# One-hot operands of an expert layer read from PSUM, and three GpSimd steps moved out of its dense part

## The chip, the cores and the metric

The kernel runs on one core of a Trainium2 chip. The metric is the time of one execution on the device, in microseconds (us). The engines are the matrix engine (PE), VectorE (DVE), ScalarE (ACT), GpSimd (POOL) and SyncE (SP), which issues the transfers. Each has a program of its own, and they meet through semaphores. PE, DVE and ACT reach PSUM, where the matmuls write; POOL works on SBUF alone.

## What is computed

A layer of phase attention on x (2 x 4096 tokens, 256 features) is followed by a layer of 16384 small experts. The second one is what matters here:

```
x  = x + layernorm(attention(layernorm(x)))
xn = layernorm(x)
q  = xn @ Wq + bq                        # 8 heads, two halves of 32 each
v1, i1 = top_k(q1 @ K1.T, 10); v2, i2 = top_k(q2 @ K2.T, 10)
vals, best = top_k(v1[:, None] + v2[None, :], 10)
expert_idx = (i1 * 64 + i2)[best]
h  = gelu(xn . W_down[expert_idx]) * softmax(vals)
x  = x + layernorm(sum(h * W_up[expert_idx]))
```

## The kernel before

The attention phase comes first and ends near 0.8 ms. `experts_phase` then takes the 8192 tokens in 32 chunks of C = 256. Its loop is a software pipeline that each engine's program writes out by hand: iteration m runs the dense layer of chunk m, builds the gate matrix of chunk m + 1, makes the lists of chunk m + 2 and starts chunk m + 3. What an engine's loop body says in which order is the order in which it works.

No expert is gathered. The indices that occur lie below 4096, and each is split into a number q (128 values, NQ) and a number r (32 values, NR). The dense layer computes all experts for all tokens of the chunk in 16 pairs of r: `down` on PE (12 matmuls a pair, into one of two banks, `hbank[p % 2]`), `gelu` on ACT from that bank into `hid`, `mix` on POOL, which multiplies by the gates, and `up` on PE, three pairs later. x and the weights are split into a high and a low part for `down`, hence `xT_hi` and `xT_lo`.

The gates of a chunk come from one-hots over its 80 slots (8 heads x 10): for each token, PE multiplies a one-hot of q (`ohq`, 80 x 128) with one of r that carries the gate (`ohr`, 80 x 32, a high and a low part). The 256 tokens are four blocks of 64. The q one-hots of block 0 are made by POOL (`onehots`, 13 pieces beside the pairs), those of block 1 by ACT, those of blocks 2 and 3 by DVE (`onehots_q`, 8192 elements a partition). DVE makes all r one-hots (`onehots_r`: a comparison, a product with `ghi`, a product with `glo`, 2048 elements each). A comparison sets a number per token against `q_no`, a row of the numbers 0 to 127. All of it is fp16.

In iteration m DVE runs, in this order: the moments of chunk m + 3, `decode` of chunk m + 1 (splits the indices, and makes the factors of POOL's one-hots), the lists of m + 2 (`lists_first`, `lists_rest`, `pair_sums`, whose first sum has 160 elements, `pairs_top`, `shift`, `mask`, `product`), then `onehots_r` and `onehots_q` of m + 1 with `finish` and `norm_out` of m between them, and `soften`. PE runs the dense layer, then the queries and scores of m + 3, and the four blocks of gate matmuls; block b waits for DVE's r one-hots of that block.

POOL runs `root(0, m + 3)` (a reciprocal root for the input's norm, two instructions on 2 elements a partition), then the 16 pairs: `mix`, and beside it `add_input` (the residual of chunk m - 1) at pair 0, `low_x` (x's low part, chunk m + 2) at pair 1, `norm_in` (the norm itself, chunk m + 3) at pair 2, `low_gates` at pair 5, `numbers` and `pair_numbers` at pair 10, and a piece of `onehots` in each of 13. At the end it runs `root(1, m)`, for the output's norm.

Of the kernel before, what the change touches and what calls it, by code (L numbers as in the profile page):

```python
# [5 lines left out]
F32, F32R, F16, BF16, U16 = mybir.dt.float32, mybir.dt.float32r, mybir.dt.float16, mybir.dt.bfloat16, mybir.dt.uint16  # L6
# [16 lines left out]
BLOCKS = 4  # L23
# [772 lines left out]
def experts_phase(nc, ctx, sems, chunks, x1_dram, out_dram, w, x1_written):  # L796
# [77 lines left out]


    consts_in, wq_in, wdown_in, wup_in, x1_in, x1t_in, out_done = (
        sem(f"b_{n}") for n in ("consts_in", "wq_in", "wdown_in", "wup_in", "x1_in", "x1t_in", "out"))
# [16 lines left out]
        sem(f"b_{n}") for n in ("q_no", "eid", "fields", "qid", "id16", "oh16"))  # L894
    ohr_eq_done, ohr_hi_done, ohr_lo_done, ohq_done = (sem(f"b_{n}") for n in ("ohr_eq", "ohr_hi", "ohr_lo", "ohq"))

    xT_done, xT_hi_done, q_done, score_done, exp_done, picked_done, gateT_done, ghi_done = (
        sem(f"b_{n}") for n in ("xT", "xT_hi", "q", "score", "exp", "picked", "gateT", "ghi"))
    gates_done, wd_hi_done, gelu_done, rid_done, minus_qid_done, distance_done, ohq_act_done = (
        sem(f"b_{n}") for n in ("gates", "wd_hi", "gelu", "rid", "minus_qid", "distance", "ohq_act"))  # L900

# [88 lines left out]
    def pool_program(pool):  # L990
# [51 lines left out]
        def low_gates(m):  # L1042
            pool.wait_ge(ghi_done, m + 1)
            if m:
                pool.wait_ge(ohr_lo_done, BLOCKS * m)
            G.tensor_tensor(glo[:, :, :], twice(gateT[:, :]), ghi[:, :, :], ALU.subtract).then_inc(glo_done, 1)
# [23 lines left out]
        for m in range(-3, chunks + 1):  # L1070
            if has(m + 3):
                root(0, m + 3)

            if m in (-2, -1):
                for p in range((m + 2) * PAIRS_R // 2, (m + 3) * PAIRS_R // 2):
                    low_down(p)
            for p in range(PAIRS_R):
                if has(m):
                    mix(m, p)
                if p == 0 and has(m - 1):  # L1080
                    add_input(m - 1)
                if p == 1 and has(m + 2):
                    low_x(m + 2)
                if p == 2 and has(m + 3):
                    norm_in(m + 3)
                if p == AT_GLO and has(m + 1):
                    low_gates(m + 1)
                if p == AT_CID and has(m + 2):
                    numbers(m + 2)
                    pair_numbers(m + 2)  # L1090
                if p < POOL_PARTS and has(m + 1):
                    onehots(m + 1, p)
            if has(m):
# [142 lines left out]
    def act_program(act):  # L1236
# [29 lines left out]
        def turn_gates(m):  # L1266
            act.wait_ge(gate_pe, m + 1)
            if m:
                act.wait_ge(glo_done, m)
            S.mul(gateT[:, :], mbank[1][0:SLOTS, 0:C], GATE_SCALE).then_inc(gateT_done, 1)  # L1270
            act.wait_ge(gateT_done, m + 1)
            if m:
                act.wait_ge(ohr_hi_done, BLOCKS * m)
            S.copy(ghi[:, :, :], gateT[:, :].unsqueeze(2).to_broadcast([SLOTS, C, 2])).then_inc(ghi_done, 1)
# [25 lines left out]
        def soften(m):  # L1300
# [50 lines left out]
        for m in range(-3, chunks + 1):  # L1351
# [30 lines left out]
    def dve_program(dve):  # L1382
# [8 lines left out]
        def onehots_q(m, b):  # L1391
            tok = slice(b * BLK, (b + 1) * BLK)
            shape = [SLOTS, BLK, NQ // 2, 2]
            dve.wait_ge(q_no_done, 1)
            dve.wait_ge(qid_done, m + 1)
            if m:
                dve.wait_ge(gates_pe, GROUPS * m)
            V.tensor_tensor(ohq[:, tok, :].rearrange("p n (q s) -> p n q s", s=2),  # L1398
                            qid[:, tok, :].unsqueeze(2).to_broadcast(shape),
                            q_no[0:SLOTS, :].rearrange("p (q s) -> p q s", s=2).unsqueeze(1).to_broadcast(shape),  # L1400
                            ALU.is_equal).then_inc(ohq_done, 1)

# [188 lines left out]
        for m in range(-3, chunks + 1):  # L1591
# [106 lines left out]
```

## Time and profile before

| | before |
|---|---|
| median of 3 executions | 3560.59 us (3557.9 to 3568.86) |
| profiled execution | 3565.71 us, span 3563.9 us |
| busy | PE 3177.3 us (89%), DVE 3086.5 (87%), ACT 2120.2 (59%), POOL 1935.4 (54%) |
| mean granted clock of PE | 0.891 |

The span runs from the first to the last instruction of the profiled execution. Busy shares are means over two phases with different limits: in the expert phase alone the page shows PE and DVE in nine tenths or more of nearly every slice.

### The profile page before, as it was taken

How to read it: one execution, taken by the hardware profiler on the slowest of the kernel's cores; microseconds unless marked ns; L12 is line 12 of the kernel's file. 1: busy time of each engine (PE TensorE's matmuls, PEld its weight loads, DVE VectorE, ACT ScalarE, POOL GpSimd, SP SyncE). 2: the span in 40 equal slices, each digit the busy share in tenths (PEclk: the TensorE clock that was granted, in tenths of full speed). 3: DMA queues.
4: the chain of work that ended last, by engine and by line, in shares of the span. 5: the costliest groups of instructions: out<-in, count | busy, mean ns of one | idle time of the engine just before them, and what ended most of it. 6: DMA issues, size and time to landing. Idle time of an engine off the chain costs nothing. (4 is left out here: it accounts for less than half of the span.)

```text
span 3563.9 us, 91251 instructions
## 1 busy us (share of the span) xinstructions
PE 3177.3 (89%) x31284; PEld 2733.0 (77%) x31284; DVE 3086.5 (87%) x15020; ACT 2120.2 (59%) x4411; POOL 1935.4 (54%) x1758
## 2 busy tenths in 40 slices
PE   5999999972599999999999999999999999999988
PEld 3666666642488888888888888888888888888878
DVE  5666666656999999999999999999999999999971
ACT  3444444422666666666666766666666666766662
POOL 1333333333466666556556666666556656666664
PEclk9999999986699988988888999889998888999988
DMA  2111111103333333333333333333333333333332
GB/s 64 48 54 54 54 54 54 42 30 133 141 117 117 116 105 114 122 105 105 105 105 118 125 119 119 117 108 105 124 112 105 105 105 115 124 124 117 114 117 95
DMA packets 132328, 356.85 MB, mean 100 GB/s; under 512 B 13865, under 2 KB 61609, under 8 KB 129452
## 3 DMA queue, kind: packets, MB, share of 16 engines
q1 hardware_dynamic: 131868, 351.03, 30.3%
q8 instruction: 251, 4.11, 0.5%
q14 instruction: 209, 1.71, 0.2%
HBM read 309.01 MB, written 25.17 MB: 94 GB/s over the span
## 5 line engine op out<-in xcount | busy, mean ns | idle before, releaser
L1209 PE MATMUL b_ps_a<-b_wup,b_hid 128*128 128x256 f32 x4096 | 955.8, 379 | 1.5 <-POOL b_hid L1023 1.5
L1198 PE MATMUL b_ps_h<-b_xT_hi,b_wd_split 128*128 128x256 f32 x4096 | 931.9, 311 | 22.7 <-ACT b_hid L1349 22.5
L1209 PEld LDWEIGHTS b_ps_a<-b_wup,b_hid 128*128 128x128 f32 x4096 | 744.3, 190 | 85.7 <-POOL b_hid L1023 1.7
L1023 POOL TENSOR_TENSOR b_hid<-b_hid,b_gates 128x512 f32<-128x512 f32 x512 | 661.9, 1295 | 197.8 <-ACT b_hid L1349 197.8
L1198 PEld LDWEIGHTS b_ps_h<-b_xT_hi,b_wd_split 128*128 128x128 f32 x4096 | 703.5, 200 | 38.3 <-issue 27.9
L1328 ACT ACTIVATE b_ohq<-b_q_no,b_minus_qid 80x128 f16<-80x128 f16 x2048 | 648.7, 391 | 1.0
L1004 POOL TENSOR_SCALAR b_rstd<-b_mv 128x2 f32<-128x2 f32 x64 | 136.4, 2131 | 860.8 <-DVE b_mv L1388 860.8
L1123 PE MATMUL b_ps_s<-b_ohr,b_ohq 80*128 80x32 f16 x16384 | 452.6, 185 | 167.1 <-issue 125.5
L1198 PE MATMUL b_ps_h<-b_xT_lo,b_wd_split 128*128 128x256 f32 x2048 | 596.9, 291 | 0.0
L1123 PEld LDWEIGHTS b_ps_s<-b_ohr,b_ohq 80*128 80x128 f16 x16384 | 443.8, 102 | 176.0 <-issue 132.3
L1349 ACT ACTIVATE b_hid<-b_ps_h 128x512 f32<-128x512 f32 x512 | 303.8, 593 | 371.5 <-PE b_ps_h L1198 371.3
L1038 POOL TENSOR_TENSOR b_ohq<-b_qT 80x640 f16<-80x640 f16 (+1 forms) x416 | 519.8, 1250 | 0.0
L1244 ACT ACTIVATE b_gates<-b_ps_s 128x512 f32<-128x512 f32 x512 | 298.1, 595 | 245.8 <-PE b_ps_s L1123 243.9
L1198 PEld LDWEIGHTS b_ps_h<-b_xT_lo,b_wd_split 128*128 128x128 f32 x2048 | 412.0, 201 | 9.9
L1336 ACT ACTIVATE b_ohq<-b_ohq,b_one 80x1024 f16<-80x1024 f16 x256 | 291.6, 1139 | 0.1
L1398 DVE TENSOR_TENSOR b_ohq<-b_qid,b_q_no 80x8192 f16<-80x8192 f16 x64 | 284.0, 4438 | 0.2 <-issue 0.2
L240 POOL TENSOR_TENSOR a_ret<-a_prod 128x512 f32<-128x512 f32 x64 | 84.9, 1327 | 329.7 <-DVE a_prod L618 329.7
L1519 DVE TENSOR_TENSOR b_cand<-b_val 128x80 f32<-128x80 f32 (+3 forms) x160 | 219.6, 1435 | 2.9
L1485 DVE FIND_INDEX8 b_idx<-b_val,b_score 128x8 uint16<-128x64 f32 x1024 | 200.4, 218 | 0.0
L1500 DVE FIND_INDEX8 b_idx<-b_val,b_score 128x8 uint16<-128x64 f32 x1024 | 200.4, 219 | 0.0
L1492 DVE MATCH_REPLACE8 b_score<-b_val,b_score 128x64 f32<-128x64 f32 x1024 | 199.8, 209 | 0.0
L480 ACT COPY a_carry<-a_ps_c 32x512 f32<-32x512 f32 x128 | 68.0, 576 | 216.9 <-PE a_ps_c L336 216.7
(192 smaller groups left out, 5508.8 us busy)
## 6 DMA issues: line engine op xcount, KB each, us to landing
b_wd_split<-wd_parts SPq DMA_DIRECT2D x512, 512.0 KB, 3.8
a_keysh<-a_key SPq DMA_DIRECT2D x16, 896.0 KB, 5.4
a_x<-in_x SPq DMA_DIRECT2D x16, 512.0 KB, 4.9
x_between<-a_y SPq DMA_DIRECT2D x16, 512.0 KB, 3.2
b_x<-x_between SPq DMA_DIRECT2D x32, 256.0 KB, 2.7
wd_parts<-b_wd_split SPq DMA_DIRECT2D x16, 512.0 KB, 2.9
b_x1t<-x_between SPq DMA_DIRECT2D x32, 256.0 KB, 5.5
out<-b_y SPq DMA_DIRECT2D x32, 256.0 KB, 5.6
```

The lines of the kernel that those rows point to most:

```text
L1023: G.tensor_tensor(hid[:, p % 4, :, :], hid[:, p % 4, :, :], gates[:, 2 * p:2 * p + 2, :], ALU.mult).then_inc(mix_done, 1)
L1038: G.tensor_tensor(ohq[:, tok, :].rearrange("p n (a b) -> p n a b", a=16), oh16[:, tok, :].unsqueeze(3).to_broadcast(shape), oh8[:, tok, :] ...
L1123: mm = T.matmul(bank[:, n * NR:(n + 1) * NR], ohq[:, tok, :], ohr[:, b % 2, tok - b * BLK, part, :], start=part == 0, stop=part == 1)
L1198: mm = T.matmul(hbank[p % 2][:, j * C:(j + 1) * C], a, c, start=i == 0, stop=i == len(parts) - 1)
L1209: mm = T.matmul(abank[:, t * D:(t + 1) * D], hid[:, p % 4, j, t * P:(t + 1) * P], wup[:, 2 * p + j, :], start=p == 0 and j == 0 and t == 0 ...
L1244: S.mul(gates[:, :, g * GROUP:(g + 1) * GROUP], sbank[fills["gates", m, g] % 3][:, :].rearrange("p (n r) -> p r n", r=NR), 1.0 / GATE_SCAL ...
L1328: op = S.activation(ohq[:, BLK + i, :], q_no[0:SLOTS, :], ACT.Abs, bias=minus_qid[:, i:i + 1])
L1336: S.activation(rows, rows, ACT.Relu, bias=one[:, :], scale=-1.0).then_inc(ohq_act_done, 1)
L1349: S.activation(hid[:, p % 4, :, :], hbank[p % 2][:, :].rearrange("p (j c) -> p j c", j=2), ACT.Gelu).then_inc(gelu_done, 1)
L1398: V.tensor_tensor(ohq[:, tok, :].rearrange("p n (q s) -> p n q s", s=2), qid[:, tok, :].unsqueeze(2).to_broadcast(shape), q_no[0:SLOTS, :] ...
L1485: op = V.max_index(idx[:, t, l, 0:8], val[:, t, l, 0:8], src(l))
L1519: op = V.tensor_tensor(cand[:, :, off:off + na * nb].rearrange("p h (a b) -> p h a b", a=na), v[:, :, 0, a0:a0 + na].unsqueeze(3).to_broad ...
```

## The change

DVE's one-hots take their small operands from PSUM in place of SBUF. The two banks of `down` are free once the activations of a chunk are done, so a part of the first one receives a copy of `q_no` (`keep_q_numbers`, on DVE, once per chunk) and the second one copies of `ghi` and `glo` (`keep_gate_parts`, on ACT, after `turn_x`). The copies move 4-byte words, and the one-hots read them as fp16. On POOL the norm of the input (`norm_in`) moves right behind its root, ahead of the dense layer; `low_x` moves behind the 16 pairs and takes chunk m + 3; `add_input` moves behind `root(1, m)` and takes chunk m.

```diff
+    q_no_ps = hbank[0][0:SLOTS, :].bitcast(F16)[:, 0:NQ]
+    gate_ps = [hbank[1][0:SLOTS, :].bitcast(F16)[:, i * 2 * C:(i + 1) * 2 * C].rearrange("p (n s) -> p n s", s=2) for i in range(2)]
...
         def low_gates(m):
             pool.wait_ge(ghi_done, m + 1)
             if m:
-                pool.wait_ge(ohr_lo_done, BLOCKS * m)
+                pool.wait_ge(gate_ps_done, m)
...
             if has(m + 3):
                 root(0, m + 3)
+                norm_in(m + 3)
...
-                if p == 0 and has(m - 1):
-                    add_input(m - 1)
-                if p == 1 and has(m + 2):
-                    low_x(m + 2)
-                if p == 2 and has(m + 3):
-                    norm_in(m + 3)
...
+            if has(m + 3):
+                low_x(m + 3)
             if has(m):
                 root(1, m)
+                add_input(m)
...
-            if m:
-                act.wait_ge(ohr_hi_done, BLOCKS * m)
             S.copy(ghi[:, :, :], gateT[:, :].unsqueeze(2).to_broadcast([SLOTS, C, 2])).then_inc(ghi_done, 1)
...
+        def keep_gate_parts(m):
+            act.wait_ge(glo_done, m + 1)
+            if m:
+                act.wait_ge(gelu_done, PAIRS_R * m)
+
+            for i, part in enumerate((ghi, glo)):
+                op = S.copy(hbank[1][0:SLOTS, i * C:(i + 1) * C], part[:, :, :].rearrange("p n s -> p (n s)").bitcast(F32))
+            op.then_inc(gate_ps_done, 1)
...
             if has(m + 3):
                 turn_x(m + 3)
+            if has(m + 1):
+                keep_gate_parts(m + 1)
+            if has(m + 3):
                 queries(m + 3)
...
-            dve.wait_ge(q_no_done, 1)
+            dve.wait_ge(q_no_ps_done, m + 1)
...
-                            q_no[0:SLOTS, :].rearrange("p (q s) -> p q s", s=2).unsqueeze(1).to_broadcast(shape),
+                            q_no_ps.rearrange("p (q s) -> p q s", s=2).unsqueeze(1).to_broadcast(shape),
                             ALU.is_equal).then_inc(ohq_done, 1)
...
+        def keep_q_numbers(m):
+            dve.wait_ge(q_no_done, 1)
+            if m:
+                dve.wait_ge(gelu_done, PAIRS_R * m - 1)
+            V.tensor_copy(hbank[0][0:SLOTS, 0:NQ // 2], q_no[0:SLOTS, :].bitcast(F32)).then_inc(q_no_ps_done, 1)
...
-            dve.wait_ge(glo_done, m + 1)
-            V.tensor_tensor(hi, lo, ghi[:, tok, :].unsqueeze(2).to_broadcast(shape), ALU.mult).then_inc(ohr_hi_done, 1)
+            dve.wait_ge(gate_ps_done, m + 1)
+            V.tensor_tensor(hi, lo, gate_ps[0][:, tok, :].unsqueeze(2).to_broadcast(shape), ALU.mult).then_inc(ohr_hi_done, 1)
             dve.wait_ge(ohr_hi_done, n + 1)
-            V.tensor_tensor(lo, lo, glo[:, tok, :].unsqueeze(2).to_broadcast(shape), ALU.mult).then_inc(ohr_lo_done, 1)
+            V.tensor_tensor(lo, lo, gate_ps[1][:, tok, :].unsqueeze(2).to_broadcast(shape), ALU.mult).then_inc(ohr_lo_done, 1)
...
             if has(m + 1):
+                keep_q_numbers(m + 1)
                 onehots_r(m + 1, 0)
```

On POOL, from one iteration into the next, there stands before: the root of the output (L1004 and L1007, of which the last one is the first row), the root of the next input, and then the pairs with their guests (`mix` is L1023, `onehots` L1038).

```order
L1007 TENSOR_TENSOR b_rstd<-b_rstd,b_minus_half 128x2
L1004 TENSOR_SCALAR b_rstd<-b_mv 128x2
L1007 TENSOR_TENSOR b_rstd<-b_rstd,b_minus_half 128x2
L1023 TENSOR_TENSOR b_hid<-b_hid,b_gates 128x512
L1012 TENSOR_TENSOR b_y<-b_y,b_x1t 128x512
L1038 TENSOR_TENSOR b_ohq<-b_qT 80x640
L1023 TENSOR_TENSOR b_hid<-b_hid,b_gates 128x512
L997 TENSOR_TENSOR b_xT_lo<-b_xT,b_xT_hi 128x512
L1038 TENSOR_TENSOR b_ohq<-b_qT 80x640
L1023 TENSOR_TENSOR b_hid<-b_hid,b_gates 128x512
L1028 TENSOR_SCALAR b_x1<-b_x1,b_mv,b_rstd 128x256 x2
```

And in the changed kernel, from the last three products of an iteration on (`mix` is L1028 there, `onehots` L1043, `low_x` L1002, `add_input` L1017, `norm_in` L1033).

```order
L1028 TENSOR_TENSOR b_hid<-b_hid,b_gates 128x512 x3
L1002 TENSOR_TENSOR b_xT_lo<-b_xT,b_xT_hi 128x512
L1009 TENSOR_SCALAR b_rstd<-b_mv 128x2
L1012 TENSOR_TENSOR b_rstd<-b_rstd,b_minus_half 128x2
L1017 TENSOR_TENSOR b_y<-b_y,b_x1t 128x512
L1009 TENSOR_SCALAR b_rstd<-b_mv 128x2
L1012 TENSOR_TENSOR b_rstd<-b_rstd,b_minus_half 128x2
L1033 TENSOR_SCALAR b_x1<-b_x1,b_mv,b_rstd 128x256 x2
L1028 TENSOR_TENSOR b_hid<-b_hid,b_gates 128x512
L1043 TENSOR_TENSOR b_ohq<-b_qT 80x640
```

The residual, x's low part and the norm have left the pairs and stand around them, four instructions in all.

On DVE, behind `product` (L1569), there stands before the first r block and the start of the second: a comparison (L1412), the product with the high part (L1417) and with the low part (L1419).

```order
L1569 TENSOR_TENSOR b_score<-b_score,b_cid 128x4320
L1412 TENSOR_TENSOR b_ohr<-b_rid,b_q_no 80x64x32
L1417 TENSOR_TENSOR b_ohr<-b_ohr,b_ghi 80x64x32
L1419 TENSOR_TENSOR b_ohr<-b_ohr,b_glo 80x64x32
L1412 TENSOR_TENSOR b_ohr<-b_rid,b_q_no 80x64x32
```

And in the changed kernel (`product` is L1590 there).

```order
L1590 TENSOR_TENSOR b_score<-b_score,b_cid 128x4320
L1422 COPY b_ps_h<-b_q_no 80x64
L1433 TENSOR_TENSOR b_ohr<-b_rid,b_ps_h 80x64x32
L1438 TENSOR_TENSOR b_ohr<-b_ohr,b_ps_h 80x64x32
L1440 TENSOR_TENSOR b_ohr<-b_ohr,b_ps_h 80x64x32
```

The copy is new, and one of the two inputs of each one-hot is now `b_ps_h`, a bank of PSUM, in the other r blocks and in the q one-hots too. Nothing else of DVE's order moves: the same instructions follow each other, with the copy ahead of the first r block.

## Rows read from the trace of the kernel before

Rows of a timeline give the start in us, the duration in us, the engine, the line, the operation with output and inputs, and the idle time before it in brackets with what ended it. Rows of groups end in count, busy us, mean ns of one, and idle time before them.

**Rows 1.** Windows: stretch, length, busy us and instructions by engine, clock, DMA

```profile
1869.54:1951.99 82.45, 76.44 (x891) 70.50 (x888) 81.19 (x432) 55.77 (x123) 51.10 (x46) 0.89 0.36 113
1923.30:1951.99 28.69, 23.61 (x560) 21.26 (x559) 28.21 (x36) 17.33 (x29) 6.79 (x4) 0.75 0.13 47
```

**Rows 2.** Timeline of PE at the end of one iteration

```profile
1944.03 3.58 PE L1123 MATMUL b_ps_s<-b_ohr,b_ohq 80*128 80x32 f16 x128 [2.78 <-issue]
1948.58 3.57 PE L1123 MATMUL b_ps_s<-b_ohr,b_ohq 80*128 80x32 f16 x128 [0.97 <-issue]
1951.99 0.56 PE L1198 MATMUL b_ps_h<-b_xT_hi,b_wd_split 128*128 128x256 f32 x1
```

**Rows 3.** Timelines of DVE, first and twelfth of thirty such rows

```profile
990.59 6.14 DVE L1519 TENSOR_TENSOR b_cand<-b_val 128x160 f32<-128x160 f32 x1
...
1898.77 6.50 DVE L1519 TENSOR_TENSOR b_cand<-b_val 128x160 f32<-128x160 f32 x1
```

**Rows 4.** Timeline of POOL beside the last row

```profile
1898.88 1.29 POOL L1023 TENSOR_TENSOR b_hid<-b_hid,b_gates 128x512 f32<-128x512 f32 x1
...
1905.16 0.35 POOL L1054 TENSOR_SCALAR b_id<-b_idx 128x160 f16<-128x160 uint16 x1
```

**Rows 5.** Groups of DVE by line and shape, 1200 to 3500 us

```profile
L1398 DVE TENSOR_TENSOR b_ohq<-b_qid,b_q_no 80x8192 f16<-80x8192 f16 x56 | 248.8, 4443 | 0.2 <-issue 0.2
L1519 DVE TENSOR_TENSOR b_cand<-b_val 128x160 f32<-128x160 f32 x27 | 171.8, 6364 | 2.4
...
L1412 DVE TENSOR_TENSOR b_ohr<-b_rid,b_q_no 80x2048 f16<-80x2048 f16 x113 | 140.0, 1239 | 3.7 <-issue 3.7
...
L1446 DVE TENSOR_TENSOR b_qT<-b_field,b_q_no 80x512 f16<-80x512 uint16 x28 | 19.1, 680 | 0.0
...
L1519 DVE TENSOR_TENSOR b_cand<-b_val 128x80 f32<-128x80 f32 x54 | 17.2, 318 | 0.0
```

**Rows 6.** Timeline of POOL during a q one-hot of DVE

```profile
1936.07 4.29 POOL L1004 TENSOR_SCALAR b_rstd<-b_mv 128x2 f32<-128x2 f32 x1 [17.97 <-DVE b_mv L1388]
```

**Rows 7.** Timeline of DVE beside a run of L1017 on POOL

```profile
885.15 1.74 DVE L1446 TENSOR_TENSOR b_qT<-b_field,b_q_no 80x512 f16<-80x512 uint16 x1
```

**Rows 8.** Groups of DVE in the first phase, 0 to 750 us

```profile
L605 DVE TENSOR_TENSOR a_u<-a_cs,a_ps_p 128x512 f32<-128x512 f32 x62 | 42.1, 678 | 7.0 <-PE a_ps_p L306 4.2 <-issue 2.7
...
L564 DVE TENSOR_TENSOR a_wg<-a_key,a_wg 128x1024 fp32r<-128x1024 f32 x1 | 1.2, 1218 | 0.0
...
L564 DVE TENSOR_TENSOR a_wb<-a_key,a_wb 128x256 fp32r<-128x256 f32 x1 | 0.4, 416 | 0.0
```

**Rows 9.** Groups of POOL by line and shape, 1200 to 3500 us

```profile
L1028 POOL TENSOR_SCALAR b_x<-b_x,b_mv,b_rstd 128x256 f32<-128x256 f32 x52 | 63.4, 1226 | 0.0
L1012 POOL TENSOR_TENSOR b_y<-b_y,b_x1t 128x512 f32<-128x512 f32 x28 | 37.3, 1331 | 0.0
L997 POOL TENSOR_TENSOR b_xT_lo<-b_xT,b_xT_hi 128x512 fp32r<-128x512 f32 x27 | 34.3, 1271 | 0.0
```

**Rows 10.** Timelines of ACT, then POOL: activation and product of pair 9

```profile
1979.60 0.60 ACT L1349 ACTIVATE b_hid<-b_ps_h 128x512 f32<-128x512 f32 x1 [0.35 <-PE b_ps_h L1198]
...
1983.70 1.27 POOL L1023 TENSOR_TENSOR b_hid<-b_hid,b_gates 128x512 f32<-128x512 f32 x1
```

**Rows 11.** Timeline of POOL at the start of an iteration

```profile
1950.69 0.72 POOL L1007 TENSOR_TENSOR b_rstd<-b_rstd,b_minus_half 128x2 f32<-128x2 f32 x1
```

**Rows 12.** Timelines of ACT, then DVE, around the end of the dense layer

```profile
1916.16 0.60 ACT L1349 ACTIVATE b_hid<-b_ps_h 128x512 f32<-128x512 f32 x1 [0.35 <-PE b_ps_h L1198]
...
1918.94 0.62 ACT L1257 CAST b_xT_hi<-b_xT 128x512 fp32r<-128x512 f32 x1
1925.23 0.84 ACT L1287 ACTIVATE b_qT<-b_ps_s,b_bq 128x256 f32<-128x256 f32 x2 [5.67 <-PE b_ps_s L1173]
...
1918.55 2.41 DVE L1560 TENSOR_TENSOR b_score<-b_posf,b_pair_no 128x4320 f16<-128x4320 f16 x1
```

**Rows 13.** Timeline of DVE, iteration before the last

```profile
3487.65 0.76 DVE L1459 BATCH_NORM_STATS2 b_stat<-b_ps_a 128x6 f32<-128x256 f32 x2 [14.70 <-PE b_ps_a L1209]
```

More of the change, by code:

```diff
@@ L894, in experts_phase @@
         sem(f"b_{n}") for n in ("q_no", "eid", "fields", "qid", "id16", "oh16"))
-    ohr_eq_done, ohr_hi_done, ohr_lo_done, ohq_done = (sem(f"b_{n}") for n in ("ohr_eq", "ohr_hi", "ohr_lo", "ohq"))
+    ohr_eq_done, ohr_hi_done, ohr_lo_done, ohq_done, q_no_ps_done = (
+        sem(f"b_{n}") for n in ("ohr_eq", "ohr_hi", "ohr_lo", "ohq", "q_no_ps"))
     xT_done, xT_hi_done, q_done, score_done, exp_done, picked_done, gateT_done, ghi_done = (
         sem(f"b_{n}") for n in ("xT", "xT_hi", "q", "score", "exp", "picked", "gateT", "ghi"))
-    gates_done, wd_hi_done, gelu_done, rid_done, minus_qid_done, distance_done, ohq_act_done = (
-        sem(f"b_{n}") for n in ("gates", "wd_hi", "gelu", "rid", "minus_qid", "distance", "ohq_act"))
+    gates_done, wd_hi_done, gelu_done, rid_done, minus_qid_done, distance_done, ohq_act_done, gate_ps_done = (
+        sem(f"b_{n}") for n in ("gates", "wd_hi", "gelu", "rid", "minus_qid", "distance", "ohq_act", "gate_ps"))
     xT_pe, q_pe, score_pe, picks_pe, picked_pe, gate_pe, gates_pe, down_pe, up_pe = (
@@ L1405, in onehots_r @@
             n = BLOCKS * m + b
-            dve.wait_ge(q_no_done, 1)
+            dve.wait_ge(q_no_ps_done, m + 1)
             dve.wait_ge(rid_done, m + 1)
@@ L1412, in onehots_r @@
             V.tensor_tensor(lo, rid[:, tok, :].unsqueeze(2).to_broadcast(shape),
-                            q_no[0:SLOTS, 0:NR].rearrange("p (r s) -> p r s", s=2).unsqueeze(1).to_broadcast(shape),
+                            q_no_ps[:, 0:NR].rearrange("p (r s) -> p r s", s=2).unsqueeze(1).to_broadcast(shape),
                             ALU.is_equal).then_inc(ohr_eq_done, 1)
             dve.wait_ge(ohr_eq_done, n + 1)
-            dve.wait_ge(glo_done, m + 1)
-            V.tensor_tensor(hi, lo, ghi[:, tok, :].unsqueeze(2).to_broadcast(shape), ALU.mult).then_inc(ohr_hi_done, 1)
+            dve.wait_ge(gate_ps_done, m + 1)
+            V.tensor_tensor(hi, lo, gate_ps[0][:, tok, :].unsqueeze(2).to_broadcast(shape), ALU.mult).then_inc(ohr_hi_done, 1)
             dve.wait_ge(ohr_hi_done, n + 1)
-            V.tensor_tensor(lo, lo, glo[:, tok, :].unsqueeze(2).to_broadcast(shape), ALU.mult).then_inc(ohr_lo_done, 1)
+            V.tensor_tensor(lo, lo, gate_ps[1][:, tok, :].unsqueeze(2).to_broadcast(shape), ALU.mult).then_inc(ohr_lo_done, 1)
         def decode(m):
```

## The prediction

> **What bounds the kernel now.** I read the windows first. Of the span of 3563.9 us the expert phase takes more than three quarters, and in its steady part one iteration of the loop (one chunk of 256 tokens) lasts 82.45 us, with VectorE (DVE) busy for 81.19 and the matrix engine (PE) for 76.44 [rows 1]. A busy share that high says little alone, so I asked who waits for whom. In the timeline PE waits 2.78 and 0.97 us ahead of the third and fourth block of gate matmuls, which read what DVE's one-hots write, and the dense layer of the next chunk can only start behind the fourth, at 1951.99 [rows 2]. DVE's one-hots and sums have next to no idle time ahead of them (0.2 to 3.7 us over 28 iterations, [rows 5]). So DVE's own list of instructions, end to end, sets the period, and PE would need 82.45 - 2.78 - 0.97 = 78.7 us.
>
> DVE's list holds one thing that is no work. The first sum of candidate values, 160 numbers, takes 6.50 us in the shown iteration and 6.14 in the first of thirty such rows [rows 3]; the group's mean is 6.364 us, while the next sum, of 80 numbers, takes 0.318 [rows 5]. I take the latter as its real length. While it stands there GpSimd (POOL) runs five instructions without a gap, and the sum ends just after POOL has reached L1054, where its run breaks [rows 4]. DVE is being held off by POOL: about 6.364 - 0.318 = 6.05 us of each iteration. It goes the other way too: a POOL instruction on four numbers takes 4.29 us where it starts beside a q one-hot of 4.443 us [rows 5, 6]. And where POOL runs a row of L1017, a DVE instruction that takes 0.680 us elsewhere takes 1.74 [rows 5, 7]: here DVE gets a turn after one POOL instruction, at 1.06 us each. All these DVE instructions read two tensors from SBUF. The Trainium skill, SBUF — State Buffer, section Who interferes with whom, states that a DVE instruction with two SBUF inputs contends with a POOL instruction that reads SBUF, and one with at most one such input does not; these rows agree with the first half, and none shows the second for a two-tensor operation.
>
> **The change, part by part.** Times below lie on the shown iteration.
>
> *POOL's dense-layer work.* Three pieces leave it: L1012 (1.331 us), L997 (1.271) and two of L1028 (1.226 each), together 5.05 us [rows 9]. Today POOL is late: the activation of pair 9 ends at 1980.20, the product on it starts at 1983.70, 3.5 us later [rows 10]. POOL needs about 1.26 us an instruction (five between 1898.88 and 1905.16), 2.5 us a pair; PE and ACT deliver a pair every 3.17 us (pair 9 at 1979.60, an iteration earlier at 1897.15; pair 15 at 1916.16, six pairs on) [rows 4, 10, 12]. Without 5.05 us of other work, about one of which turns into waiting for the first activations, POOL is level at pair 9, and from there it idles 0.7 us in each pair. That is where DVE's candidate sum arrives. Its hold-off shrinks from 6.05 us to what is left of one pair of POOL instructions, between 0 and 2.5; I take one turn, 1.06.
>
> *The input's norm* now runs straight behind the root at the start of the iteration. POOL's L1007 ends at 1951.41 [rows 11], and DVE is then in its decode, whose last four instructions read two SBUF tensors. Two POOL instructions fall on them. By the turn of [rows 7] that costs DVE 2 x 1.06 = 2.1 us that it doesn't pay today. Bounds: 0, and 2 x 1.226 = 2.45.
>
> *A knock-on at the end of the dense layer.* DVE reaches L1560 at 1918.55 today, when POOL is done [rows 12]. It will be there about 6.05 - 3 x 1.06 = 2.9 us sooner, at 1915.7, and run until 1918.1. The last activation ends at 1916.76 [rows 12]; POOL's product on it then queues behind L1560 and takes its turn before L1569, another two-input instruction. One more turn of 1.06 (0 to 1.27).
>
> *x's low part and the residual.* Low x waits for ACT's copy at 1919.56 [rows 12] and falls behind L1569 at the worst; nothing reads it until a later chunk. The residual runs during the last r one-hots. Both cost 0 if those one-hots, with one input now in PSUM, don't contend; if they do, 1.06 to 1.27 each.
>
> *The one-hots.* Fourteen an iteration: 2 of L1398, and 12 of L1412, L1417 and L1419. No row shows a two-byte tensor read from PSUM. The nearest: in the first phase 256 and 1024 fp32 elements take 0.416 and 1.218 us from SBUF, so 0.149 + 1.044 ns an element, which gives 0.684 for 512; the same width with one input in PSUM took 0.678 [rows 8]. So where an operand lies costs nothing there. L1412 takes 1.239 us for 2048 elements, 0.6 ns each: two-byte tensors pass two at a time [rows 5]. I take both to stay: 0 extra. The upper bound is that they pass singly, below.
>
> *The copies.* DVE copies 64 words of numbers to PSUM ahead of the first one-hot, which waits for it: 0.2 us, bounded by 0 and the 0.318 of an 80-element sum [rows 5]. ACT copies the two parts of the gates, at most 0.62 each by its nearest copy, ahead of a wait of 5.67 us for the queries [rows 12], so hidden. They are done at 1919.56 + 1.24 = 1920.8, and DVE's first multiplication, at about 1924.7 today (L1560's start plus two of 2.41 and one of 1.24), will come at about 1923. It doesn't wait. If that cover went it would cost the difference.
>
> *The end.* In the iteration before the last DVE makes one-hots early and then idles 14.70 us for PE [rows 13]. Now they must wait for the dense layer, since its banks hold their operands. The chain after the dense layer there grows by two r blocks and a q block, 6 x 1.24 + 4.44 = 11.9 us [rows 5], less some 8 that fit beside its last pairs (an estimate): about 4 us, once.
>
> *Sum.* 6.05 - 1.06 - 2.1 - 1.06 - 0.2 = 1.6 us an iteration, 30 times (the count in rows 3): 48 us, less 4 is 44. The profiled execution took 3565.7 us, 5.1 above the median 3560.6, so I expect about 3521 for a profiled one and **3517** for the median. The new period is 80.8, above PE's 78.7, so DVE still sets it.
>
> **The rivals.**
> *PE becomes the bound.* If the new collisions mostly miss (POOL idle when DVE comes), DVE falls to 82.45 - 6.05 + 0.2 = 76.6 and PE's 78.7 decides: 3.75 x 30 = 112, less 4: 3452. Half-way cases lie at 3480 to 3500. For it: POOL's gaps of 0.7 in a pair. Against it: the norm and the decode both start from the same event, so these two must meet. The chance of anything from 3452 to 3500: 0.28.
> *The bills eat the gain.* With all upper bounds, 2.5 + 2.45 + 1.27 + 0.3 = 6.5 of the 6.05, the time is 3560.6 + 0.45 x 30 + 4 = 3578. This fits if DVE is passed over for more than one turn, as in rows 3. Between 3550 and 3580: 0.18, about half of it within 0.3%.
> *A two-byte operand in PSUM passes one element at a time.* Then L1398 takes 0.149 + 8192 x 1.044 ns = 8.70 us and L1412 2.29: 2 x 4.26 + 12 x 1.05 = 21.1 us an iteration, 32 chunks: 675 us, so 3517 + 675 = 4190. It decides as soon as the one-hots, 23.8 us an iteration, grow by more than 1.5 us, 6%. Against it: the fp32 row of [rows 8], which could not show it. The chance: 0.10.
> The Trainium skill, VectorE: DVE Perf Modes, speaks for this rival: the perf-mode tier table there gives tensor_tensor one element per cycle with any PSUM operand. The section Why PSUM operands drop a tier, on the same page, leaves two-byte data two per cycle. No row here settles it.
> *The change does not free POOL* (another wait holds the candidate sum): then only the new bills show, 3578 to 3600; 0.03, since the sum ends with POOL's run in all thirty rows.
>
> **How the numbers follow.** The forecast, 3500 to 3550, has 0.41. A difference under 0.3%, 11 us, is about what a measurement of this kernel can't tell from none. Faster: 0.41 + 0.28 = 0.69; the same: 0.11; slower: 0.20, half of it by the PSUM rate. The range takes all bounds but the far cases: 3455 to 3565.
>
> **What would show it.** In the profile after, the candidate sum of 160 should average 1.4 us instead of 6.364; the decode's two-input instructions should take about 2 us more in sum; L1560 should start near 1.2 us before the last activation ends, and L1569 or the product be 1 us long in excess; L1398 should stay at 4.44 and L1412 at 1.24 (8.7 and 2.3 mean the third rival); L1004 should fall from 4.29 to about 0.2 beside a q one-hot; PE's waits ahead of the third and fourth block should shrink but not vanish. I'm wrong if the turns are longer than one POOL instruction, or if PSUM's rate is lower.

## The result, and the profile after

The median fell from 3560.64 us (3557.9 to 3568.86, four executions) to 3501.7 (3500.14 to 3502.66, four): a ratio of 0.9824 with a 95% interval of 0.9812 to 0.9836. I had said 3517, so the sign held, and the gain, 59 us, was larger than the 44 of the sum. The mechanism of the gain held too, but two terms of the sum were off by the same 1.9 us in opposite directions, as the last parts show.

The quickest way to see where it came from is one instruction that runs once per chunk. The fused field operation of `decode` is L1440 before and L1461 after. The views of those two lines (count, shortest, median and longest duration in ns, first and last start in us), before and after:

```profile
L1440 DVE SCALAR_TENSOR_TENSOR b_id<-b_eid,b_field x32: 278/280/1347, 883.9 to 3431.1; 80x128 f16<-80x128 uint16 x32
```

```profile
L1461 DVE SCALAR_TENSOR_TENSOR b_id<-b_eid,b_field x32: 279/281/282, 883.8 to 3363.8; 80x128 f16<-80x128 uint16 x32
```

Over 31 chunks 2547.2 us became 2480.0: a mean period of 82.17 against 80.00, 2.17 less. From the last start to the end of the span it was 132.8 and is 136.3, 3.5 us more. The two spans differ by 63.8 us, the medians by 59: the profiled execution of the kernel before lay 5 us above its median.

The windows of a steady iteration and of its tail (columns as in [rows 1]):

```profile
1843.02:1923.25 80.23, 76.42 (x886) 70.47 (x887) 77.00 (x433) 56.38 (x126) 51.13 (x47) 0.90 0.36 116
1895.00:1923.25 28.25, 25.42 (x569) 22.87 (x568) 25.90 (x34) 17.38 (x30) 3.86 (x6) 0.78 0.17 58
```

PE and POOL are busy as long as in [rows 1] (76.42 against 76.44, 51.13 against 51.10), and PE's granted clock is 0.90 against 0.89; VectorE's busy time fell from 81.19 to 77.00. But 80.23 - 77.00 leaves 3.2 us in which DVE is not shown busy, where before there were 1.3. The groups of DVE say which lines shrank, which grew, and where it now waits (columns as in [rows 5], 1200 to 3350 us):

```profile
L1412 DVE TENSOR_TENSOR b_ohq<-b_qid,b_ps_h 80x8192 f16<-80x8192 f16 x54 | 237.4, 4397 | 0.0
...
L1433 DVE TENSOR_TENSOR b_ohr<-b_rid,b_ps_h 80x2048 f16<-80x2048 f16 x106 | 128.5, 1213 | 51.1 <-PE b_ps_s L1126 50.1
...
L1590 DVE TENSOR_TENSOR b_score<-b_score,b_cid 128x4320 f16<-128x4320 f16 x27 | 90.9, 3368 | 0.9
...
L1540 DVE TENSOR_TENSOR b_cand<-b_val 128x80 f32<-128x80 f32 x54 | 39.1, 724 | 0.0
...
L1471 DVE TENSOR_TENSOR b_qT<-b_id,b_q_no 80x1024 f16<-80x1024 f16 x27 | 23.6, 872 | 0.0
...
L1540 DVE TENSOR_TENSOR b_cand<-b_val 128x160 f32<-128x160 f32 x27 | 13.2, 490 | 2.8 <-issue 0.4
```

The candidate sum of 160 fell from 6364 ns [rows 5] to 490. The two sums behind it grew from 318 to 724 each: part of the hold-off has moved onto them. L1590, `product`, takes 3368 ns and took 2443. The one-hots take as long with an operand in PSUM: 4397 against 4443 ns, 1213 against 1239. But [rows 5] reach to 3500 us and so into the last iterations; in the window used here the kernel before has 4402 ns for the q one-hot, 2408 for `product`, 6423 for the sum of 160, and for the r comparison

```profile
L1412 DVE TENSOR_TENSOR b_ohr<-b_rid,b_q_no 80x2048 f16<-80x2048 f16 x105 | 127.4, 1213 | 0.0
```

So where the operand lies changed nothing for the one-hots there. And L1433, the r comparison, waits 50.1 us for PE's gate matmuls: a wait that the kernel before did not have.

The timeline of POOL shows what stands beside the shorter sum (columns as in [rows 4]):

```profile
1871.18 1.28 POOL L1028 TENSOR_TENSOR b_hid<-b_hid,b_gates 128x512 f32<-128x512 f32 x1 [0.47 <-ACT b_hid L1360]
1872.41 1.34 POOL L1043 TENSOR_TENSOR b_ohq<-b_qT 80x640 f16<-80x640 f16 x1
1874.34 1.28 POOL L1028 TENSOR_TENSOR b_hid<-b_hid,b_gates 128x512 f32<-128x512 f32 x1 [0.58 <-ACT b_hid L1360]
...
1886.95 2.99 POOL L1028 TENSOR_TENSOR b_hid<-b_hid,b_gates 128x512 f32<-128x512 f32 x1 [1.22 <-ACT b_hid L1360]
1890.10 3.24 POOL L1028 TENSOR_TENSOR b_hid<-b_hid,b_gates 128x512 f32<-128x512 f32 x1 [0.17 <-ACT b_hid L1360]
...
1905.11 0.22 POOL L1009 TENSOR_SCALAR b_rstd<-b_mv 128x2 f32<-128x2 f32 x1 [10.53 <-DVE b_mv L1402]
...
1922.55 3.34 POOL L1033 TENSOR_SCALAR b_x<-b_x,b_mv,b_rstd 128x256 f32<-128x256 f32 x2
```

POOL now waits for each activation by pair 9, half a microsecond a pair, where before it ran 3.5 us behind [rows 10]. The five sums, from 1872.25 to 1874.26, lie between two of those gaps and last 2.01 us. The fourth and fifth row are products that stretch from 1.28 to about 3 us: DVE holds them. The root beside a q one-hot takes 0.22 us in its row and took 4.29 [rows 6]. The last row is the moved norm, two instructions in 3.34 us.

DVE beside these rows, in time order: the five candidate sums as one row, `product`, the copy, a q one-hot, the r comparison of block 2, and the end of `decode`:

```profile
1872.25 2.01 DVE L1540 TENSOR_TENSOR b_cand<-b_val 128x160 f32<-128x160 f32 x5
...
1888.84 3.37 DVE L1590 TENSOR_TENSOR b_score<-b_score,b_cid 128x4320 f16<-128x4320 f16 x1
1892.13 0.22 DVE L1422 COPY b_ps_h<-b_q_no 80x64 f32<-80x64 f32 x1
...
1904.93 4.38 DVE L1412 TENSOR_TENSOR b_ohq<-b_qid,b_ps_h 80x8192 f16<-80x8192 f16 x1
1911.25 1.22 DVE L1433 TENSOR_TENSOR b_ohr<-b_rid,b_ps_h 80x2048 f16<-80x2048 f16 x1 [1.93 <-PE b_ps_s L1126]
...
1922.38 0.56 DVE L1458 SCALAR_TENSOR_TENSOR b_qid<-b_eid 80x384 f16<-80x384 uint16 x1
1922.86 0.28 DVE L1461 SCALAR_TENSOR_TENSOR b_id<-b_eid,b_field 80x128 f16<-80x128 uint16 x1
1923.06 0.68 DVE L1467 TENSOR_TENSOR b_qT<-b_field,b_q_no 80x512 f16<-80x512 uint16 x1
1923.66 0.88 DVE L1471 TENSOR_TENSOR b_qT<-b_id,b_q_no 80x1024 f16<-80x1024 f16 x1
```

The row at 1911.25 is the new wait: DVE is done with the q one-hots at 1909.3 and stands for 1.93 us. `onehots_r` has two buffers, and block 2's has to be given back by PE's block 0. PE comes to that block only after the dense layer, the queries and the scores, and there it stops once more for ACT. The timeline of PE, as in [rows 2]:

```profile
1906.23 2.56 PE L1126 MATMUL b_ps_s<-b_ohr,b_ohq 80*128 80x32 f16 x96
1910.12 4.41 PE L1126 MATMUL b_ps_s<-b_ohr,b_ohq 80*128 80x32 f16 x160 [1.33 <-ACT b_gates L1247]
1915.07 3.58 PE L1126 MATMUL b_ps_s<-b_ohr,b_ohq 80*128 80x32 f16 x128 [0.54 <-issue]
1919.61 3.57 PE L1126 MATMUL b_ps_s<-b_ohr,b_ohq 80*128 80x32 f16 x128 [0.96 <-issue]
1923.02 0.56 PE L1201 MATMUL b_ps_h<-b_xT_hi,b_wd_split 128*128 128x256 f32 x1
```

PE's waits ahead of its third and fourth block fell from 2.78 and 0.97 [rows 2] to 0.54 and 0.96. So each engine waits for the other: PE for the fourth r block, DVE for the buffer of the third.

### The profile page after: what moved, and what is told of

Read it like the earlier page. It is cut to its first block and busy times, and to the rows that moved or that the text cites. A ratio compares the mean times of both kernels' runs of the same rounds, so it can differ in the third digit from the quotient of the medians.

```text
span 3500.1 us, 91378 instructions
## 1 busy us (share of the span) xinstructions
PE 3179.7 (91%) x31284; PEld 2737.6 (78%) x31284; DVE 2952.2 (84%) x15052; ACT 2138.9 (61%) x4475; POOL 1916.9 (55%) x1758
## 5 line engine op out<-in xcount | busy, mean ns | idle before, releaser
L1028 POOL TENSOR_TENSOR b_hid<-b_hid,b_gates 128x512 f32<-128x512 f32 x512 | 768.3, 1501 | 182.9 <-ACT b_hid L1360 182.5
L1043 POOL TENSOR_TENSOR b_ohq<-b_qT 80x640 f16<-80x640 f16 (+1 forms) x416 | 520.4, 1252 | 0.0
L1009 POOL TENSOR_SCALAR b_rstd<-b_mv 128x2 f32<-128x2 f32 x64 | 14.1, 221 | 518.1 <-DVE b_mv L1402 518.1
L1412 DVE TENSOR_TENSOR b_ohq<-b_qid,b_ps_h 80x8192 f16<-80x8192 f16 x64 | 281.4, 4397 | 0.0
L1017 POOL TENSOR_TENSOR b_y<-b_y,b_x1t 128x512 f32<-128x512 f32 x32 | 40.7, 1273 | 303.6 <-DVE b_y L1489 303.6
L1433 DVE TENSOR_TENSOR b_ohr<-b_rid,b_ps_h 80x2048 f16<-80x2048 f16 x128 | 155.2, 1213 | 57.1 <-PE b_ps_s L1126 56.0
```

The source lines that it names most:

```text
L1028: G.tensor_tensor(hid[:, p % 4, :, :], hid[:, p % 4, :, :], gates[:, 2 * p:2 * p + 2, :], ALU.mult).then_inc(mix_done, 1)
L1043: G.tensor_tensor(ohq[:, tok, :].rearrange("p n (a b) -> p n a b", a=16), oh16[:, tok, :].unsqueeze(3).to_broadcast(shape), oh8[:, tok, :] ...
```

## The experiments

**Each half alone.** The first kernel keeps the PSUM operands and puts POOL's order back; the second keeps POOL's new order and puts the one-hots' operands back into SBUF.

```diff
 e1: on top of the changed kernel
             if has(m + 3):
                 root(0, m + 3)
-                norm_in(m + 3)
...
+                if p == 0 and has(m - 1):
+                    add_input(m - 1)
+                if p == 1 and has(m + 2):
+                    low_x(m + 2)
+                if p == 2 and has(m + 3):
+                    norm_in(m + 3)
...
-            if has(m + 3):
-                low_x(m + 3)
             if has(m):
                 root(1, m)
-                add_input(m)
 e2: the same lines the other way, on top of the kernel before
```

> The changed kernel with POOL's order as it was before: only the operands of the one-hots lie in PSUM. Theory A (the gain comes from what left the dense layer on POOL): the candidate sum is held for 6 us again, the one-hots save at most 0.04 us each, so 3550 to 3565 us, about the time before. Theory B (the gain comes from the PSUM operands, since DVE and POOL then share less): 3510 us or less, and a candidate sum well under 6 us.

> The kernel before with only the three moves on POOL, all operands in SBUF. Theory A: the candidate sums fall to about 2 us in sum of five, as in the changed kernel. The residual now falls on the last r one-hots and low x on the first ones, which read two SBUF inputs and so can be held for one POOL instruction, about 1 us each; one of these is hidden in DVE's wait of 1.93 us for PE. So 3505 to 3535 us. Theory B: little changes, 3550 us or more.

The PSUM operands alone: 3576.84 (3570.47 to 3580.54), a ratio of 1.0041 (1.0027 to 1.0055), slightly slower than before. The moves alone: 3528.31 (3522.2 to 3529.85), 0.9905 (0.9889 to 0.9922). So 32 us come from the moves, 59 from both, and the PSUM operands cost 16 alone. In e1 two DVE groups tell it:

```profile
L1542 DVE TENSOR_TENSOR b_cand<-b_val 128x160 f32<-128x160 f32 x26 | 167.1, 6427 | 2.7 <-issue 0.4
...
L1592 DVE TENSOR_TENSOR b_score<-b_score,b_cid 128x4320 f16<-128x4320 f16 x26 | 62.6, 2408 | 0.9
```

The candidate sum is held as before, and `product` isn't held. What is left is the copy and the later start of the last chunk's one-hots. The time is a miss of the expectation, which ended at 3565; the attribution comes back to it. In e2 the sum of 160 is short, as in the changed kernel (685 ns), and the bill is at the one-hots and at the POOL steps that now lie beside them; groups of DVE, then of POOL:

```profile
L1415 DVE TENSOR_TENSOR b_ohr<-b_ohr,b_ghi 80x2048 f16<-80x2048 f16 x104 | 176.6, 1698 | 3.6
L1410 DVE TENSOR_TENSOR b_ohr<-b_rid,b_q_no 80x2048 f16<-80x2048 f16 x104 | 154.4, 1484 | 2.5 <-PE b_ps_s L1121 0.5
```

```profile
L997 POOL TENSOR_TENSOR b_xT_lo<-b_xT,b_xT_hi 128x512 fp32r<-128x512 f32 x26 | 58.5, 2248 | 0.0
L1012 POOL TENSOR_TENSOR b_y<-b_y,b_x1t 128x512 f32<-128x512 f32 x26 | 55.1, 2118 | 81.9 <-DVE b_y L1466 81.9
```

With both inputs in SBUF the two kinds of r one-hot take 1698 and 1484 ns in the mean; with one in PSUM they take 1217 and 1213. That is 4 x (0.481 + 0.271) = 3.0 us an iteration which the moves alone cost and the PSUM operands save. In a timeline of e2 it is three turns of about 1 us: the last product of `mix` and then `low_x` fall on the first two instructions of block 0, and the residual on one of block 3. The net gain of the operands on top of the moves is smaller, 80.97 - 80.00 = 0.97 us in the mean period (L1438 of e2 starts from 878.1 to 3388.3), since the changed kernel also pays the copy, 0.2, and the wait for the r buffer, 1.9, which e2 hardly has (2.5 us in all). POOL's low part takes 2248 ns there and 1272 in the changed kernel. This is the second half of the rule that the prediction cited from the Trainium skill (SBUF — State Buffer, section Who interferes with whom), that a DVE instruction with at most one SBUF input doesn't contend. No row of before could show it; these do.

**The new wait.** e3 puts block 2's r one-hots into space of `hid`, which is free from the last `up` matmul of a chunk to the first activation of the next, and block 3's into slot 0. Block 2 then waits for no block of its own chunk, and block 3 for block 0, three ahead in place of two. e4 leaves the buffers and moves `norm_out` ahead of block 2, which only fills the wait with other work.

```diff
 e3
+    ohr2 = hid[0:SLOTS, :, :, :].rearrange("p a b c -> p (a b c)").bitcast(F16).rearrange("p (n a r) -> p n a r", n=BLK, a=2)
+    ohr_block = [ohr[:, 0], ohr[:, 1], ohr2, ohr[:, 0]]
...
-            if n >= 2:
-                dve.wait_ge(gates_pe, BLOCK_GROUPS * (n - 1))
+            if b == 3:
+                dve.wait_ge(gates_pe, BLOCK_GROUPS * (n - 2))
+            elif n >= 4:
+                dve.wait_ge(gates_pe, GROUPS * m)
 e4
-                onehots_r(m + 1, 2)
             if has(m):
                 norm_out(m)
             if has(m + 1):
+                onehots_r(m + 1, 2)
                 onehots_r(m + 1, 3)
```

> The changed kernel with the r one-hots of block 2 in the space of hid, so that DVE needs no wait for PE's gate matmuls of block 0. Theory A (the wait of 1.93 us an iteration is what took back part of DVE's gain): the wait goes, PE's own 80.2 less 0.54 and 0.96 of idle time decides, 78.7 us an iteration: 3450 to 3465 us. Theory C (DVE's instructions alone set the period, the wait only fills a gap that PE would leave anyway): 3495 to 3505 us.

> The changed kernel with norm_out ahead of the r one-hots of block 2 on DVE, so that its 0.9 us fill half of the wait for PE. Theory A: 0.9 us an iteration, 30 times, 27 us less: 3468 to 3480 us, with a wait of about 1.0 in place of 1.93. Theory C: no change, 3497 to 3505 us.

e3 took 3445.72 (3444.02 to 3447.0), 0.9673 (0.9657 to 0.9689); e4 took 3474.96 (3469.57 to 3476.96), 0.9749 (0.9733 to 0.9766). The r comparison in e3, then in e4:

```profile
L1437 DVE TENSOR_TENSOR b_ohr<-b_rid,b_ps_h 80x2048 f16<-80x2048 f16 x81 | 98.2, 1212 | 0.9
```

```profile
L1433 DVE TENSOR_TENSOR b_ohr<-b_rid,b_ps_h 80x2048 f16<-80x2048 f16 x108 | 131.0, 1213 | 27.1 <-PE b_ps_s L1126 26.2
```

Idle time ahead of it: 51.1 us in the changed kernel, 27.1 in e4, 0.9 in e3, over 26 or 27 iterations. The runs lie 27 (e4) and 56 us (e3) below the changed kernel. The periods say what of that belongs to the wait. The field operation of `decode` starts from 886.7 to 3338.5 in e4 (L1461), and in e3

```profile
L1465 DVE SCALAR_TENSOR_TENSOR b_id<-b_eid,b_field x32: 278/281/282, 875.0 to 3305.1; 80x128 f16<-80x128 uint16 x32
```

These are periods of 79.09 and 78.39 us against 80.00. In e4 the wait fell by 0.9 us and the period by 0.91; in e3 the wait of 1.9 went and the period fell by 1.61. So the buffer's wait set the period of the changed kernel, down to about 78.4, where e3 meets the next bound. Another 8.8 us of the difference between the profiled executions of e3 and the changed kernel come from the earlier start of the expert phase, 875.0 against 883.8, whose code up to there is the same. Over the nine profiles that start ranges from 875.0 to 886.7, and single profiles don't tell whether that belongs to the kernel or to the execution; the mean period is the safer number. Without the 8.8 us e3's 3445.7 would lie in the 3450 to 3465 expected; as it stands it misses that range by 4.

**Is it the norm in the dense layer?** e5 takes the changed kernel and moves only `norm_in` back to pair 2.

```diff
 e5
                 root(0, m + 3)
-                norm_in(m + 3)
...
+                if p == 2 and has(m + 3):
+                    norm_in(m + 3)
```

> The changed kernel with norm_in back at pair 2 of the dense layer, everything else as changed. Theory A (DVE's candidate sum is passed over until POOL's run of instructions breaks, so what counts is whether POOL is level with the activations by then): with 2.45 us more to do, POOL is level only behind pair 10, the sum is held for about 4.5 us, of which the wait of 1.93 us for PE and the freed holds take up 3: 3530 to 3550 us. Theory D (DVE is held for one instruction of POOL's at a time): the sum is held for one turn as now, 3497 to 3505 us.

3545.83 (3545.21 to 3551.07), a ratio of 0.9954 (0.9937 to 0.9971) to before, whose median in that group of runs was 3564.19. The sum is held again; its group, then POOL's timeline at the end of the hold in one iteration, in which DVE shows `1886.36 5.81` for the five sums:

```profile
L1541 DVE TENSOR_TENSOR b_cand<-b_val 128x160 f32<-128x160 f32 x26 | 130.0, 5001 | 2.7 <-issue 0.4
```

```profile
1886.14 1.25 POOL L1043 TENSOR_TENSOR b_ohq<-b_qT 80x640 f16<-80x640 f16 x1
1887.36 1.26 POOL L1028 TENSOR_TENSOR b_hid<-b_hid,b_gates 128x512 f32<-128x512 f32 x1
1888.58 1.25 POOL L1043 TENSOR_TENSOR b_ohq<-b_qT 80x640 f16<-80x640 f16 x1
1889.80 1.28 POOL L1028 TENSOR_TENSOR b_hid<-b_hid,b_gates 128x512 f32<-128x512 f32 x1
1891.17 0.34 POOL L1059 TENSOR_SCALAR b_id<-b_idx 128x160 f16<-128x160 uint16 x1
```

Two instructions of 1.22 us put back into the dense layer, and 4.5 us of hold-off return on the first sum; the sums of 80 are back at 316 ns, so over the five sums it is 3.8. The period rose by 1.5 only (L1462 from 879.2 to 3406.9, 81.54), since the wait of 1.9 for PE is gone. DVE reaches the candidate sum while POOL is in an unbroken run, and the run of two-tensor instructions ends at L1059, where the first sum gets through, as in [rows 4]. So in this place the hold-off is not a price per POOL instruction: it lasts as long as POOL's run, and 2.5 us decide whether POOL is still in one.

**Is DVE held in `decode`, and by what?** The prediction has the norm, started beside `decode`, hold DVE by a turn for each of its two instructions. It didn't: L1471 takes 872 ns in the mean, where the same instruction (L1450) took 680 before, and the norm is the one that is held, 1674 ns each against 1226 [rows 9]. e6 puts another POOL step there, `low_x`, a two-tensor instruction, between the root and the norm, and takes it away from the end.

```diff
 e6
                 root(0, m + 3)
+            if has(m + 2):
+                low_x(m + 2)
+            if has(m + 3):
                 norm_in(m + 3)
...
-            if has(m + 3):
-                low_x(m + 3)
```

> The changed kernel with low_x (of chunk m + 2) between the root and norm_in at the start of the iteration, where DVE decodes. Theory E (a tensor_tensor of POOL with two inputs takes a turn from DVE, the tensor_scalar of norm_in did not): a two-input instruction of the decode takes 1.06 us more; time about the same, since the wait for PE takes it up, 3497 to 3507 us. Theory F (a chain of DVE's that runs already is not broken by a POOL instruction that asks later, whatever it is): the decode takes no more than the 0.2 us it lost in the changed kernel.

3499.29 (3497.95 to 3500.64), 0.982 (0.9803 to 0.9836): the same time. The view of L1462, the field operation shown at the top, then DVE's instruction ahead of it, and the timeline of POOL beside it:

```profile
L1462 DVE SCALAR_TENSOR_TENSOR b_id<-b_eid,b_field x32: 279/1364/1370, 881.8 to 3360.9; 80x128 f16<-80x128 uint16 x32
```

```profile
1919.95 0.56 DVE L1459 SCALAR_TENSOR_TENSOR b_qid<-b_eid 80x384 f16<-80x384 uint16 x1
...
1919.98 1.66 POOL L1002 TENSOR_TENSOR b_xT_lo<-b_xT,b_xT_hi 128x512 fp32r<-128x512 f32 x1
1921.63 3.51 POOL L1033 TENSOR_SCALAR b_x<-b_x,b_mv,b_rstd 128x256 f32<-128x256 f32 x2
```

Here DVE does pay a turn: 1364 ns against 280, 1.08 us, the size of [rows 7]. And the norm behind it is again held by DVE, 3.51 us for two. Who came first doesn't tell the two cases apart. `low_x` starts 0.03 us behind a two-tensor instruction of DVE (1919.98 and 1919.95), and the norm of the changed kernel 0.17 behind the same one (1922.55 and 1922.38). What differs is the POOL instruction: the one with two tensors made DVE wait a turn, the one with a single tensor did not. This is one pair of cases, and the reason is not shown.

The time stayed for two reasons. DVE still waits 46.4 us in all for the r buffer (50.1 in the changed kernel, over the same window), so the same loop sets the period, 79.97. And the 1.08 us came back: the sums of 80 take 271 ns (724 in the changed kernel), and L1472 677 (872).

The trace of the kernel before has one more case, at the start of the expert phase, where POOL splits weights (L1017) while DVE is in `decode`:

```profile
883.44 8.69 POOL L1017 TENSOR_TENSOR b_wd_split<-b_gates,b_wd_split 128x512 fp32r<-128x512 f32 x6
```

POOL runs six two-tensor instructions here without a gap, and yet DVE's three two-tensor instructions beside them take 1.35, 1.74 and 1.74 us (starts at 883.88, 885.15 and 886.82), a turn each: the engines alternate. So a hold that lasts to the end of POOL's run is what the candidate sum shows, and not a rule for every place.

**What bounds it after the third buffer.** In e3 PE's only wait of size in the tail is 1.33 us for ACT, which exponentiates chunk m + 2 (`soften`, with two table loads) just ahead of emptying the gate banks. e8 is e3 with `soften` moved ahead of the queries, into ACT's 5.1 us of waiting.

```diff
 e8, on top of e3
             if has(m + 1):
                 keep_gate_parts(m + 1)
+            if has(m + 2):
+                soften(m + 2)
...
-            if has(m + 2):
-                soften(m + 2)
```

> The kernel with the third r buffer, and ACT's soften (an exponential and two table loads, 3.1 us) moved ahead of queries, where ACT waits 5.1 us for PE. PE's wait of 1.33 us for ACT in block 0 should go. Theory G (in the kernel with the third buffer DVE's list and PE's are nearly level, DVE at 78.4 and PE at 78.5): the period falls by 0.1 us only: 3438 to 3446 us, and PE waits about 1.2 us for DVE's one-hots again. Theory H (PE alone decides there): 77.2 us an iteration, 3405 to 3412 us.

3443.26 (3441.36 to 3448.64), 0.9667 (0.9651 to 0.9683): no different from e3. The timeline of PE in e8:

```profile
1881.84 5.34 PE L1128 MATMUL b_ps_s<-b_ohr,b_ohq 80*128 80x32 f16 x204
1887.35 3.58 PE L1128 MATMUL b_ps_s<-b_hid,b_ohq 80*128 80x32 f16 x128 [0.17 <-issue]
1891.88 3.58 PE L1128 MATMUL b_ps_s<-b_ohr,b_ohq 80*128 80x32 f16 x128 [0.96 <-issue]
```

The wait for ACT is gone, and PE waits instead for DVE's last block, 0.96 us. In e3's timeline it ran through its last two blocks without a wait. So in e3 PE and DVE are nearly level: taking 1.33 us from PE alone gives 0.23 us an iteration (the starts of L1465 run from 875.0 to 3305.1 in e3 and from 879.0 to 3302.0 in e8, 78.39 and 78.16 in the mean, one profile each). This is the kernel with the lowest median here, 121 us below the kernel before in the same group of runs, and e3 alone has nearly all of it, 115.

## Why the prediction was right, and where its terms were off

Per iteration, term by term, in the group means of before (1200 to 3500 us) and after (1200 to 3350). Means of before in the shorter window would move no term by more than 0.1:

| term | predicted | measured |
|---|---|---|
| the five candidate sums | -6.05 + 1.06 = -5.0 | 7.56 to 2.43: -5.1 |
| `decode` beside the norm | +2.1 | +0.2 |
| `product` beside the last activation's product | +1.06 | 2.443 to 3.368: +0.93 |
| the copy | +0.2 | +0.21 |
| `shift` (L1576, now L1597) | not seen | 602 to 326 ns: -0.3 |
| DVE's wait for the r buffer | not seen | 50.1 us over 27: +1.9 |
| sum | -1.6 | -2.2 |

The measured terms add up to -2.2, and the mean period fell by 2.17. Two of them show that the number came out near the forecast in part by luck: `decode` cost 1.9 us less than priced, and the wait for the r buffer, which had no price, cost 1.9. With `decode` priced right and the wait still at nothing, the sum would have been 3.5 us an iteration, a period close to PE's 78.7, and about 3460 us. The measured 3501.7 lies 1.7 us inside the forecast's 3500 to 3550. The extra gain, 15 us by the medians and 20 by the spans, comes from small terms: 0.3 us an iteration from `shift`, 0.1 each from the candidate sums and `product`, and 31 periods where the sum took 30. The "7.56" is 6.364 + 2 x 0.318 with 0.297 and 0.265 for the sums of 64 and 48 elements, the "2.43" the same lines after.

*The candidate sum*: right in mechanism and size. POOL, relieved of 5 us, is level with ACT by pair 9, as worked out; e5 shows that 2.5 us of the five already decide it. I had put the whole rest of the hold-off on the first sum (1.4 us in the mean); it is 0.49 there, and the rest lies on the sums of 80. (The POOL instruction of 4.29 us that the prediction says is on four numbers is the root, on two numbers a partition; nothing hangs on it.)

*`decode`*: this step failed. The text said, of the norm, "Two POOL instructions fall on them. By the turn of [rows 7] that costs DVE 2 x 1.06 = 2.1 us". It costs 0.2. The turn was read from a row beside L1017, an instruction with two tensors, and carried over to one that reads a single tensor. e6 puts a two-tensor one there and finds the 1.08. The range from 0 to 2.45 held it; the choice between the ends was wrong.

*`product`*: right in kind and size, but not by the instruction that I named. The last activation, and the DVE instruction that I expected to start 1.2 us before its end:

```profile
1889.43 0.60 ACT L1360 ACTIVATE b_hid<-b_ps_h 128x512 f32<-128x512 f32 x1 [0.35 <-PE b_ps_h L1201]
...
1886.39 2.41 DVE L1581 TENSOR_TENSOR b_score<-b_posf,b_pair_no 128x4320 f16<-128x4320 f16 x1
```

L1581 starts 3.6 us before that end, since DVE is earlier than the sum had it. So POOL's product of the last pair but one (the row at 1886.95) queues behind L1581 and takes its turn before L1590, which is 0.93 longer; the last pair's then waits for L1590. In e1, where POOL is still late, `product` (L1592) takes 2408.

*The copies and ACT*: right. ACT copies at 1892.73 and 1893.04 and then waits 5.10 us for the queries.

*The PSUM rate*: the third rival is out, with 4397 ns where it gave 8700. The perf-mode tier table (Trainium skill, VectorE: DVE Perf Modes), which has one element per cycle for tensor_tensor with any PSUM operand, doesn't hold for this form, two-byte elements with one operand in SBUF and one in PSUM: 2048 elements take 1.213 us here and took 1.213 from SBUF alone in the same window. The section Why PSUM operands drop a tier, which leaves two-byte data two per cycle, is the one that agrees.

*The end*: 4 us forecast, 3.5 measured. In the iteration before the last the copy waits for the activations, and a product for ACT's copies:

```profile
3409.05 0.22 DVE L1422 COPY b_ps_h<-b_q_no 80x64 f32<-80x64 f32 x1 [43.78 <-ACT b_hid L1360]
...
3413.93 1.22 DVE L1438 TENSOR_TENSOR b_ohr<-b_ohr,b_ps_h 80x2048 f16<-80x2048 f16 x1 [3.41 <-ACT b_ps_h L1316]
```

*What bounds the kernel next*: this step failed too, and it hid behind the first. I wrote "DVE still sets it", with PE's 78.7 as the next bound. With `decode` costing 0.2 instead of 2.1 DVE's own list needs 80.0 - 1.9 = 78.1 us (e3, without the wait, has a period of 78.4), and that is below a third bound that I hadn't priced: a loop over both engines, from PE's gate block 0 through the r buffer to DVE's blocks 2 and 3 and back to PE's block 3, hung onto the end of PE's scores. It stands at 80.0. All of the 1.9 us that `decode` gave was taken back there. The first rival (PE the bound, 3452 to 3500) was missed by 2 us for that reason, and e3, which takes only that loop away, lands at 3445.7. PE's wait ahead of the third block shrank as forecast, from 2.78 to 0.54; the one ahead of the fourth stayed (0.97 and 0.96).

*The attribution*: the prediction treats the two halves as one. The runs separate them: without the moves the PSUM operands gain nothing, and without the PSUM operands the moves lose 3.0 us an iteration at the one-hots. e1 took 3576.8 where 3550 to 3565 was expected. Of its 16 us above the kernel before its trace shows 10 (0.19 us in each of 31 periods and 4.2 at the end); the other 6 are not explained by any row. The two profiled executions differ by 6.1 us only: e1's expert phase starts 3.8 us earlier, its total lies 4.8 below its median, and the other's lies 5.1 above.

## What to carry to other kernels

When two engines hold each other off, the hold is not in proportion to the work beside it, so look where the other engine's run begins and ends: 2.5 us of POOL's work put back cost DVE 3.8 us at its candidate sums (e5), and 1.3 us moved elsewhere cost nothing in all (e6). Take the price of a collision only from a row where the same kind of instruction (two inputs or one, in the same place) met the same kind, and keep the full range otherwise. Before naming the next bound, go through each buffer with few slots whose writer is the engine that gets faster: its wait is at zero before and so stands in no list of waits.

## What the runs showed of the hardware

- A DVE instruction on two SBUF tensors was passed over for up to five POOL instructions in a row in the candidate sum, to the end of POOL's run (6.36 us in the mean before, 5.00 in e5), but for one only in `decode` (1.08 us in e6, and three times in a row beside the run of L1017 before). The other way round POOL's products waited for DVE's `product` (1.28 us became 3.24), and the norm for `decode` (3.34 and 3.51 for two). Why DVE gets its turn after one instruction in `decode` and not in the candidate sum no run here tells, and it stays open. In the cases with one turn DVE was already in a chain of two-tensor instructions when POOL's came, and in the long ones POOL was in its run when DVE's came; no run tests whether that decides.
- With one of its inputs in PSUM a DVE one-hot neither held POOL (0.22 us for the root, 4.29 before; 1.27 for the residual, 2.12 in e2) nor was held by it (1.21 and 1.22 us, against 1.48 and 1.70 in e2).
- The same one-hots ran at the same rate with an operand in PSUM and without: 4397 and 4402 ns for 8192 two-byte elements a partition, 1213 and 1213 for 2048.
